# Expert products in plain fp32, two slots at once on the two halves of the array

## What is computed

```
t = layernorm(x)                                  # 384 x 1024
route_prob = softmax(t @ switch_w + switch_b)     # 8 experts, the best one is taken
for e in range(8):
    h = gelu(t @ w1[e] + b1[e])                   # w1[e] 1024 x 512
    y = h @ w2[e] + b2[e]                         # w2[e] 512 x 1024
    out = where(routes == e, y, out)
x = x + out * route_prob_max
```

## Time and profile before

| | |
|---|---|
| median of 3 runs | 610.32 us (609.53 to 612.1) |
| profiled execution | 610.84 us, span 609.1 us |
| TensorE busy, matmuls | 569.4 us (93%) |
| VectorE busy | 465.3 us (76%) |
| ScalarE busy | 315.6 us (52%) |
| moved by DMA | 104.21 MB, mean 171 GB/s |
| experts, first product to last | 503.7 to 597.7 us |

### The profile page before, as it was taken

The page is one execution under the profiler, slowest core; times in us unless marked ns, Lnnn a source line. Parts: engine busy times, 40 slices in busy tenths (PEclk is TensorE's granted clock), DMA queues, the critical chain, the costliest instruction groups (busy, mean ns, idle before and its releaser), DMA issues.

```text
span 609.1 us, 9044 instructions
## 1 busy us (share of the span) xinstructions
PE 569.4 (93%) x3108; PEld 517.1 (85%) x3108; DVE 465.3 (76%) x828; ACT 315.6 (52%) x476; POOL 150.8 (25%) x164
## 2 busy tenths in 40 slices
PE   3989999999999999999999999999989998898975
PEld 3889998888999999999789999999968887676763
DVE  6678887837685457743488988889798968899996
ACT  4635553320333343534176566665765443999980
POOL 5617665643274400540000010010020200000020
PEclk9989999999999999999999999999999969999998
DMA  8646468510454644477331344253574304899974
GB/s 302 223 115 193 146 186 232 180 40 1 128 158 136 214 139 137 139 223 208 104 103 70 103 109 132 70 138 138 174 199 154 128 11 138 285 415 412 411 275 174
DMA packets 33828, 104.21 MB, mean 171 GB/s; under 512 B 5472, under 2 KB 9760, under 8 KB 33792
## 3 DMA queue, kind: packets, MB, share of 16 engines
q1 hardware_dynamic: 28224, 89.95, 43.1%
q0 software_dynamic: 5424, 13.29, 8.3%
q10 hardware_dynamic: 144, 0.52, 0.3%
HBM read 96.58 MB, written 5.60 MB: 168 GB/s over the span
## 4 chain that ended last, share of the span: by engine, by line
PE 69%; DVE 17%; ACT 5%; DMA 4%; issue 4%; POOL 1%; DVEq 0%; SPq 0%; ACTq 0%
PE ps L1648 38%; DVE wsp L959 6%; PE ps L1662 5%; PE ps L1841 5%; DVE big L959 4%; PE ps L1795 3%; PE ps L1785 2%; PE ps L1938 2%; PE ps L1770 2%; PE ps L1732 2%; PE ps L1713 2%; PE ps L1805 2%; DMA raw<-in_w_experts 1%; PE ps L2013 1%; DMA tw<-in_type_weights 1%
## 5 line engine op out<-in xcount | busy, mean ns | idle before, releaser
L1648 PE MATMUL ps<-big,wsp 128*128 128x384 f32 x1656 | 297.6, 337 | 4.7 <-DVE wsp L959 3.5
L1648 PEld LDWEIGHTS ps<-big,wsp 128*128 128x128 f32 x1656 | 287.5, 189 | 9.7 <-issue 5.5
L959 DVE TENSOR_TENSOR wsp<-raw,wsp 128x1024 fp32r<-128x1024 f32 x117 | 149.8, 1295 | 33.6 <-ACT wsp L618 29.5
L618 ACT ACTIVATE wsp<-raw 128x1024 fp32r<-128x1024 f32 x83 | 87.0, 1053 | 32.9 <-PE ps L1662 12.9
L530 POOL DMA_INDIRECT edge_table<-ef,eidx x48 | 55.9, 1165 | 35.3 <-DMA edge_table<-ef,eidx 23.9
L625 ACT ACTIVATE big<-ps,bias 128x384 f32 x24 | 14.0, 584 | 81.1 <-PE ps L1648 81.1
L959 DVE TENSOR_TENSOR big<-raw_x,big 128x1024 fp32r<-128x1024 f32 x36 | 42.1, 1221 | 0.3 <-ACT big L800 0.3
L970 DVE SCALAR_TENSOR_TENSOR big<-ps,bias,big 128x384 f32 (+1 forms) x24 | 14.8, 617 | 33.7 <-ACT big L625 33.0
L742 ACT ACTIVATE work<-work,snm 128x384 f32<-128x384 f32 x48 | 29.0, 607 | 17.9 <-DVE snm L1226 17.9
L800 ACT ACTIVATE wsp<-raw 128x1024 fp32r<-128x1024 f32 x34 | 34.5, 1051 | 5.7 <-DMA raw<-in_w_experts 3.1
L2013 PE MATMUL ps<-wsp,big 128*128 128x512 f32 x112 | 29.0, 400 | 8.3 <-DVE big L959 8.3
(11 more groups left out here) (261 smaller groups left out, 846.8 us busy)
## 6 DMA issues: line engine op xcount, KB each, us to landing
raw<-in_w_stream SPq DMA_DIRECT2D x85, 512.0 KB, 3.5
raw<-in_w_experts SPq DMA_DIRECT2D x32, 512.0 KB, 6.5
raw_x<-in_w_experts SPq DMA_DIRECT2D x32, 512.0 KB, 6.1
rowbuf<-in_rowb POOLq DMA_DIRECT2D x6, 512.0 KB, 6.7
raw_x<-in_w_stream SPq DMA_DIRECT2D x4, 512.0 KB, 7.1
slot_y<-rowbuf POOLq DMA_DIRECT2D x7, 256.0 KB, 6.0
tok<-in_x SPq DMA_DIRECT2D x3, 512.0 KB, 4.0
edges_a<-in_src_rows SPq DMA_DIRECT2D x8, 192.0 KB, 4.0
```

The lines of the kernel that those rows point to most:

```text
L618: nc.scalar.activation(wsp[:, 0, slot, :], raw[:, slot, :], ACT.Copy).then_inc(w_hi, 1)
L959: return nc.vector.tensor_tensor(dst, value, hi.bitcast(F32), ALU.subtract)
L1648: ins = nc.tensor.matmul(ps[:, bank, 0:N], wsp[:, a, slot, k * P:(k + 1) * P], moving[:, b, k, :], start=(k == 0 and n == 0), stop=(k == K ...
```

## The change

The experts' weights are no longer split. Slots are worked in four pairs, and each expert product is plain fp32: slot 2p has its 64 tokens as the stationary columns whose output goes to PSUM partitions 0 to 63, slot 2p+1 those whose output goes to partitions 64 to 127, each with its own expert's weights as the moving rows. Both accumulate into the same PSUM bank, which the bias product (fp32r, 128 columns, both slots) opens. The blocks go from memory straight into 30 homes of 512 KB (`HOMES`) laid over the buffers of the stages before; those that no longer hold anything are filled during the projection with wo, and the other 34 loads wait until the block 30 places before was read. The gathered tiles hold the sum of high and low part, accumulated in PSUM, so there are eight; ScalarE copies them all. VectorE copies y, one 128 x 512 half at a time, and GpSimd writes pairs of slots. The order of the stages is up 0, up 1, down 0, up 2, down 1, down 2, up 3, down 3, and the first half of the permutation products stands inside the last down. The transposes of the hidden values and the permutation products are plain fp32, as the latter were.

```diff
+HOMES = (16, 17, 28, 29, 0, 1, 2, 3, 4, 8, 5, 9, 6, 10, 12, 13, 14, 15, 7, 11, 18, 21, 19, 22, 20, 23, 24, 27, 34, 35)
...
+STAGES = [("up", 0), ("up", 1), ("down", 0), ("up", 2), ("down", 1), ("down", 2), ("up", 3), ("down", 3)]
+BLOCKS = [b for kind, p in STAGES for b in (up_blocks(p) if kind == "up" else down_blocks(p))]
...
-            def load_expert(row, k, split):
-                sp.wait_ge(w_lo, split)
-                sp.dma_start(raw_slot(k), w_experts[bass.ds(row, P), :]).then_inc(raw_in[k], 16)
+            def load_block(b):
+                h, row = b % len(HOMES), BLOCKS[b] * P
+                sp.dma_start(blocks[:, HOMES[h], :], w_experts[row:row + P, :]).then_inc(blk_in[h], 16)
+            for b in (0, 1):
+                load_block(b)
+            sp.wait_ge(w_started, Q_WO)
+            for b in (2, 3):
+                load_block(b)
             for j in range(RING):
-                load_expert(j * P, j, Q_MOE + j - XRING + 1)
-            with sp.Fori(0, EXPERTS - 1) as i:
-                for k in range(XRING):
-                    row = sp.snap(i * (QE * P) + first * P)
-                    load_expert(row, (RING + k) % XRING, i * XRING + (Q_MOE + RING + k - XRING + 1))
+                sp.wait_ge(w_lo, Q_WO + j + 1)
+                load_block(4 + j)
+            for j in range(RING - 1):
+                sp.wait_ge(w_started, Q_WO + j + 2)
+                load_block(8 + 2 * j)
+                load_block(9 + 2 * j)
             for j in range(RING):
+                sp.wait_ge(w_lo, Q_WO + RING + j + 1)
+                load_block(14 + j)
+            for j in range(RING):
+                sp.wait_ge(w_started, Q_WO + RING + j + 1)
+                load_block(18 + 2 * j)
+                load_block(19 + 2 * j)
+            sp.wait_ge(wo_ready, 2 * NT)
+            for b in range(26, len(HOMES)):
+                load_block(b)
+            for b in range(len(HOMES), len(BLOCKS)):
+                sp.wait_ge(blk_read, b - len(HOMES) + 1)
+                load_block(b)
...
+            for p in range(TWOS - 1):
+                pool.wait_ge(y_sum, 2 * p + 2)
+                if p:
+                    pool.wait_ge(y_out, 16 * p)
+                pool.dma_start(ys_dram[p * P:(p + 1) * P, :], y_buf[p % 2]).then_inc(y_out, 16)
             pool.wait_ge(pos_done, 1)
             over = pool.value_load(rowi[0:1, OVER:OVER + 1], min_val=0, max_val=OVER)
+            pool.wait_ge(blk_read, len(BLOCKS) - len(HOMES) + NT)
+            pool.wait_ge(y_out, 16 * (TWOS - 1))
+            for t in range(NT):
                 rows_back(t)
...
+            def got(k):
+                act.wait_ge(got_ready, k + 1)
+                nc.scalar.activation(xs[:, k, :], ps[:, got_bank(k), :], ACT.Copy).then_inc(got_done, 1)
+            def copy_up(p):
+                act.wait_ge(blk_read, read_after("up", p))
+                nc.scalar.activation(u_buf, ps[:, p % 2, :], ACT.Copy).then_inc(u_copied, 1)
+            def hidden(p):
+                act.wait_ge(ht_ready, p + 1)
+                nc.scalar.activation(h_buf[p % 2], ps[:, 2, :], ACT.Gelu_apprx_tanh).then_inc(ht_act, 1)
             for k in range(KT):
+                got(k)
             act.wait_ge(perm_ready, 1)
             nc.scalar.activation(perm, ps[:, 3, 0:N], ACT.Copy).then_inc(perm_set, 1)
+            for p in range(TWOS):
+                copy_up(p)
+                hidden(p)
...
+            def y_rows(p, h):
+                dve.wait_ge(blk_read, read_after("down", p, 2 * h + 2))
+                if p >= 2 and h == 0 and p < TWOS:
+                    dve.wait_ge(y_out, 16 * (p - 1))
+                nc.vector.tensor_copy(y_buf[p % 2][:, h * HALF:(h + 1) * HALF], ps[:, y_bank(p, h), :])\
+                    .then_inc(y_sum, 1)
...
+            positions()
+            routes()
+            for p in range(TWOS - 1):
+                for h in range(2):
+                    y_rows(p, h)
+            y_rows(TWOS - 1, 0)
+            for t in range(2):
+                rows_added(t, 1, mixed)
+            dve.wait_ge(mixed, 2)
+            perm_rows_added(0, 0, 2)
+            y_rows(TWOS - 1, 1)
+            rows_added(2, 1, mixed)
+            dve.wait_ge(mixed, NT)
+            perm_rows_added(0, 2, NT)
+            perm_rows_added(1, 0, NT)
+            dve.wait_ge(perm_added, 2 * NT)
...
+            def products(bank, stationary, ks, last):
+                rows = two_blocks()
+                for kk, k in enumerate(ks):
+                    for s in range(2):
+                        ins = nc.tensor.matmul(ps[s * SLOT:(s + 1) * SLOT, bank, :], stationary(k, s),
+                                               rows[s][:, kk * HALF:(kk + 1) * HALF],
+                                               start=False, stop=(last and kk == 1))
+                        if kk == 1:
+                            ins.then_inc(blk_read, 1)
+            def up(p, between=None):
+                nc.tensor.matmul(ps[:, p % 2, :], two_hot(p), b12r[:, 0:F], start=True, stop=False)
+                for j in range(RING):
+                    if j == 2 and between:
+                        between()
+                    if p == 0:
+                        pe.wait_ge(got_done, 2 * j + 2)
+                    products(p % 2, lambda k, s: slot_x(k, 2 * p + s), (2 * j, 2 * j + 1), j == RING - 1)
+            def hidden(p):
+                pe.wait_ge(u_copied, p + 1)
+                for k in range(F // P):
+                    ins = nc.tensor.transpose(ps[:, 2, k * P:(k + 1) * P], u_buf[:, k * P:(k + 1) * P], ident)
+                ins.then_inc(ht_ready, 1)
+            def down(p, between=None):
+                pe.wait_ge(ht_act, p + 1)
+                if p >= 2:
+                    pe.wait_ge(y_sum, 2 * (p - 1))
+                for h in range(2):
+                    nc.tensor.matmul(ps[:, y_bank(p, h), :], two_hot(p), b12r[:, F + h * HALF:F + (h + 1) * HALF],
+                                     start=True, stop=False)
+                    for j in range(2):
+                        if (h, j) == (1, 1) and between:
+                            between()
+                        products(y_bank(p, h), lambda k, s: h_buf[p % 2][:, k * P + s * SLOT:k * P + (s + 1) * SLOT],
+                                 (2 * j, 2 * j + 1), j == 1)
...
-            for e in range(EXPERTS - 1):
-                up(e + 1, e + 1, RING, (lambda: hidden(0)) if e == 0 else None)
-                down(e, e, 0)
-                hidden(e + 1)
-            down(EXPERTS - 1, EXPERTS - 1, RING)
+            up(0)
+            pe.wait_ge(pos_done, 1)
+            for p in range(TWOS - 2):
+                up(p + 1, lambda: hidden(p))
+                down(p, (lambda: hidden(TWOS - 2)) if p == TWOS - 3 else None)
+            down(TWOS - 2)
+            up(TWOS - 1)
+            hidden(TWOS - 1)
+            pe.wait_ge(perm_set, 1)
+            down(TWOS - 1, lambda: permuted(0))
+            permuted(1)
```

More of the change, by code:

```diff
@@ L128, in sem @@
             return ctx.enter_context(nc.semaphore(name))
+        with nc.sbuf_tensor("blocks", [P, UNITS, D], F32) as blocks:
+            pass
         raw = sb("raw", [P, RING, D])
@@ L1344, in _ @@
             head_sum(0)
[L1345 to L1346 removed]
+            then(nc.vector.memset(kp_row.bitcast(F32), 0.0))
             pt_part(1, 5)
@@ L1578, in _, with perm_rows_added @@
+            def perm_rows_added(h, first, last):
+                cols = slice(h * HALF, (h + 1) * HALF)
+                for t in range(first, last):
                     dve.wait_ge(perm_out, h * NT + t + 1)
@@ L1980, in up_bias @@
-            def up_bias(s, e):
-                nc.tensor.matmul(ps[:, e % 2, :], slot_hot(s), b12r[:, 0:F], start=False, stop=True)\
-                    .then_inc(up_ready, 1)
-            def up(s, e, base, between=None):
-                for j in range(4):
-                    if between and j == 2:
-                        between()
-                    up_block(s, e, base, j)
-                up_bias(s, e)
-            def hidden(e):
-                pe.wait_ge(u_copied, u_no.add())
-                for k in range(F // P):
-                    ins = nc.tensor.matmul(ps[:, 2, ((e % 2) * 4 + k) * SLOT:((e % 2) * 4 + k + 1) * SLOT],
-                                           u_buf[e % 2][:, k * P:(k + 1) * P], fold, start=True, stop=True)
-                ins.then_inc(ht_ready, 1)
@@ L2060, in _, with late_product @@
             with pe.If(over > 0):
+                pe.wait_ge(perm_added, 2 * NT)
+                def late_product(o, bank, hot_bias, stationary, first, last):
+                    nc.tensor.matmul(ps[0:SLOT, bank, :], two_hot(0)[:, 0:SLOT].bitcast(F32), hot_bias.bitcast(F32),
+                                     start=True, stop=False)
+                    for j in range(first, last):
+                        pe.wait_ge(blk_in[j], 16 * (loads_of(j) + o + 1))
+                        for kk in range(2):
```

(4 more changed lines are left out.)

409 lines of the change are left out of this document (120 added, 289 removed).

## The result

The changed kernel takes 587.37 us, median of four runs (585.65 to 588.1), beside 611.21 (609.53 to 614.5) for the kernel before: a ratio of 0.96, with a 95% interval of 0.9552 to 0.9647. The execution profiled took 588.1 us, its span 586.3.

The account below looks back on a forecast made before the run. VectorE was taken to bound the kernel. Experts starting at 508.5 us plus 68.2 on TensorE gave 576.7; the tail brought the span to 586.2, and 1.7 more gave 588 us, range 582 to 610.

Parts of the forecast that it names:

- VectorE was the bound and leaves it: Experts: VectorE, busy 21.00 of 21.00 us, sets the pace; without the splits it is mostly idle from 510 us on.
- 0.43 us for a product: Experts on TensorE: column halves overlap fully, so 128 products at 0.43 us take 54.9 us; full overlap had chance 0.66.
- Rivals 1 to 3: Expert products: halves not overlapping, 642 us (chance 0.18); one load exposed each, 600 to 612 (0.13); no load overlapping, 614 to 637 (0.03).
- rival 2: Expert products: halves overlap with one load exposed per product, 0.53 to 0.62 us each, 600 to 612 us; chance 0.13.
- Start of the experts at 508.5: End of the gathers on TensorE: resumed at 497.38 us, 44 left plus 3 transposes, so experts start at 508.5.
- The sum of 68.2 us: Experts on TensorE: products, biases, transposes, permutations, fourth handoff and mode changes take 68.2 us, ending at 576.7.
- The changes between array and halves: Experts on TensorE: some 30 changes between full array and halves at 0.15 us each, 4.5 us.
- The tail of 9.5 us: Behind the last expert product: VectorE's copy and adds until 581.5, then 4.7 us for the output, ending at 586.2.
- The supply costs nothing: Expert weight blocks: thirty homes fill early, the other 34 land by 555, ahead of TensorE; no cost.
- the stream, 43 us for 34 blocks: Weight loads behind the first thirty: 34 blocks follow the reads from about 510, take 43 us, landed by 555.
- the side calculation "end near 602": Weight supply: if all thirty homes were empty at 508.5, the stream would need 81 us, the end near 602.
- The third pair's rows cost nothing: End of the experts: third pair's rows land 13.5 to 16.5 us behind its down, wanted only after the last product; no cost.

Follow-up runs that it names:

- e2_in_turn: Changed kernel with all products of one half in a stage (or half a down), then all of the other: 630.71 us, ratio 1.0319.
- e4: Changed kernel with no expert block asked for until the eighth gathered tile is copied: 618.08 us, ratio 1.0107.
- e5: Changed kernel with no expert block asked for before the projection with wo is done: 592.28 us, ratio 0.9663.
- e3: Changed kernel with up 3 moved ahead of down 2, so the third pair finishes behind the fourth's up: 591.02 us, ratio 0.9669.
- e7: Changed kernel with down biases added by VectorE while copying y, held in two of the 30 homes: 585.91 us, again 585.92.
- e6_bias_on_halves: Changed kernel with each fp32r bias product replaced by two plain fp32 products on the column halves: 593.15 us, ratio 0.9711.
- e10_free_writes: e7 with a pair's write no longer waiting until the write before it has landed: 587.63 us, ratio 0.9619.

## Why the prediction was right, point by point

**VectorE was the bound and leaves it.** Right: 1.38 of 12.00 us busy in the experts. One reading on the way was off: the row shows three slices at 411 to 415 GB/s, not four; nothing in the sum uses it.

**0.43 us for a product.** Right in size: the chain has 57.4 us on the products, and without the 0.15 us at each of 17 entries into the halves that is the 54.9 of the term. e2_in_turn shows 0.86 without the overlap. The mechanism in the prediction was wrong: I let records of the halves pass one another only in program order, the second record of one half beside the first of the other. The runs show a reach of about four records. The price came out right since the order as changed needs only one; the reach, which makes the order matter so little, was not foreseen. Rivals 1 to 3 are refuted: loads come in pairs 0.43 us apart (0.215 on average), where rival 2 wanted 0.26 to 0.31. The 2.38 times that the Trainium skill has for three column tiles (TensorE: Matmul & The Clock Gate, Part 3, measured speedup), 0.79 of ideal, would have made 0.54 us, an estimate from it; two halves measured 7.01 / 3.58 = 1.96 times.

**Start of the experts at 508.5.** Measured 506.9 in the profiled execution, of which 1.9 us lie in unchanged code: TensorE resumed the gathers at 495.43, not 497.38. From there I had 11.1 us and it took 11.5. The other traces of changed kernels start at 508.4 to 511.3, so the profiled execution was an early one.

**The sum of 68.2 us.** It measured 69.3. The changes between array and halves, priced at 4.5 us, come to about 5.4: 0.15 us for each of 17 entries, 0.21 for each of ten biases behind the halves (a bias stands with 0.43 on the chain) and 0.25 for the one behind the handoff, with another 0.5 around the transposes and the permutation products. Four transposes take 0.59 where 0.52 were priced, the last four 0.66. The fourth handoff took 2.0 us (563.11 to 565.16) with 0.66 of transposes in it, so 1.4 exposed against 1.5.

**The tail of 9.5 us.** Measured 10.1 (576.21 to the span's end): the steps of VectorE to the last add as forecast, the output 0.7 us longer.

**The supply costs nothing.** Right, with less room than I wrote: done near 560, not 555. The step that was mis-sized is the stream, 43 us for 34 blocks, which left out the table on the same DMA engines. In the changed kernel these are three writes, 1.57 MB or 3.8 us at 411 GB/s; its reads come behind the stream, at 561.5. In e4, where the reads fall into the stream too, it is 3.15 MB, and the side calculation "end near 602" failed by 16 us for it, for the products behind the last wait, and for a later start. The reserve that the homes give is real: 4 us are lost if the filling starts only behind the projection (e5), 30 if it starts with the experts (e4).

**The third pair's rows cost nothing.** Right for the changed kernel. e3 shows what they cost one stage later. In e7 they are late as well: TensorE is done 3.5 us sooner, and the reads are issued 56.9 us after the first bias instead of 54.4, since the DMA engines have more to move.

What the forecast rests on held: the halves overlap, TensorE is the new bound, and neither the blocks nor the rows hold it up. Only its picture of how records of the halves pass one another did not. That 588 fits the profiled execution so closely is luck: the errors nearly cancel, 1.9 us of an earlier start against 0.4 in the gathers, 1.1 in the experts and 0.6 in the tail. The changed kernel's second trace, which starts its experts at 511.2, took 591.37, still inside the range.

## What to carry to other kernels

Plain fp32 work with 64 columns each belongs on the two column halves with the instructions in turn, or a few records apart at most; here a half on its own paid the full stream, and without the interleaving nothing of the gain was left. Before it is counted, the stream that feeds two halves must be costed with all that shares its DMA engines, and the last wait with the products behind it. When two chains and the transfers end within a microsecond or two of one another, an edit that shortens one of them measures as nothing, so look at which wait appears next before building it.

## What the runs showed of the hardware

- Products on the two column halves overlap further than strict program order allows: in e2_in_turn 32 records took 12.22 us instead of 13.3 and 16 took 5.35 instead of 6.45, about four records of reach.
- Going from the full array to plain fp32 products on the halves costs 0.15 us, behind fp32r biases and behind plain fp32 transposes alike (3.58 instead of 3.43 us for 16 records, e6_bias_on_halves). Going back costs 0.21 for an fp32r bias (0.43 instead of 0.22), and 0.19 for six records of plain fp32 permutation products (2.77 where 6 x 0.43 is 2.58). So the change from halves to the full array costs about this much even where the type stays the same.
- In e3_third_pair_late TensorE was idle for 3.64 us; the granted clock was 0.53 over the next six records (1.2 of 2.4 GHz for most), which took 5.42 us instead of 2.84.
- A 512 KB write beside a full weight stream lands late: the third pair's took from 554.87 to 563.08, 8.2 us, in e10_free_writes. In the changed kernel the first two took 7.0 and 7.3 us beside the stream, and the third, at the stream's end, 4.0; 256 KB took 5.8 before.
